# A two-layer cross-attention and FFN kernel: the first stage written out, its key projections four batches ahead of its query projections

## The reference

```python
x = x + _L0_xattn_ref(_layernorm(x), ctx_1024, ctx_1024, ...)   # q@Wq.T+bq, k@Wk.T+bk, v@Wv.T+bv, softmax over keys, @Wo.T+bo
x = x + _L0_ffn_ref(_layernorm(x), ...)                         # router over 32+8 experts, top 6, SiLU-gated experts
x = x + _L1_xattn_ref(_layernorm(x), ctx_1024, ctx_1024, ...)   # the same with -scale
x = x + _L1_ffn_ref(_layernorm(x), ...)                         # 256 -> 704 -> 256, activations and weights rounded to FP4 blocks
```

## Time and profile before

| | us |
|---|---|
| median of 3 runs | 1002.08 (996.93 to 1007.60) |
| the profiled execution, its own time | 1005.61 |
| its span, first to last instruction | 1003.8 |
| PE busy | 898.1 (89%) |
| DVE busy | 626.4 (62%) |
| ACT busy | 437.4 (44%) |
| POOL busy | 304.1 (30%) |

### The profile page before, as it was taken

One profiled execution on the slowest core, in us unless ns is written; L12 is line 12 of the kernel. 1 busy time (PEld: TensorE's weight loads), 2 busy tenths in 40 slices (PEclk: granted clock), 3 DMA queues, 4 the chain that ended last, 5 costly groups with the idle time before them and its releaser, 6 DMA issues.

```text
span 1003.8 us, 19829 instructions
## 1 busy us (share of the span) xinstructions
PE 898.1 (89%) x7228; PEld 685.1 (68%) x7228; DVE 626.4 (62%) x1317; ACT 437.4 (44%) x946; POOL 304.1 (30%) x311
## 2 busy tenths in 40 slices
PE   2997799999997978999999967799999996699996
PEld 1764687878876747878888844587878874366664
DVE  3455577878854594545545465566777764678872
ACT  0442466666664561111111112466666675345442
POOL 8003466767782260000000004000000001476673
PEclk9998799999998798999999977999999999999998
DMA  9788644444333469121111204345565500000000
GB/s 258 219 238 203 113 93 92 93 93 93 62 106 98 138 214 250 46 67 32 32 32 48 65 3 82 74 85 112 107 117 109 106 27 21 0 11 16 16 10 22
DMA packets 98157, 90.45 MB, mean 90 GB/s; under 512 B 43554, under 2 KB 85410, under 8 KB 97954
## 3 DMA queue, kind: packets, MB, share of 16 engines
q1 hardware_dynamic: 98066, 89.25, 36.6%
HBM read 69.36 MB, written 19.63 MB: 89 GB/s over the span
## 4 chain that ended last, share of the span: by engine, by line
PE 72%; DVE 12%; DMA 5%; POOL 3%; ACT 3%; issue 2%; SPq 2%; DVEq 0%; POOLq 0%; ACTq 0%
PE ps L988 13%; PE ps L805 8%; PE ps L859 8%; PE ps L791 8%; PE ps L994 7%; PE ps L819 7%; PE ps L1062 3%; DMA Qz<-mT 3%; PE ps L709 3%; PE ps L1078 2%; PE ps L868 2%; POOL Pr L645 2%; PE ps L779 2%; PE ps L828 1%; DMA X<-x_in 1%
## 5 line engine op out<-in xcount | busy, mean ns | idle before, releaser
L1444 DVE TENSOR_REDUCE ext<-ps 112x2 f32<-112x750 f32 x256 | 232.6, 933 | 66.5 <-PE ps L791 63.4
L1175 ACT ACTIVATE Pr<-ps 125x448 f32<-125x448 f32 x384 | 199.2, 542 | 88.5 <-PE ps L805 75.0
L805 PE MATMUL ps<-Qz,Kp 98*125 98x224 f16 x768 | 130.7, 265 | 14.0 <-DMA Qz<-mT 11.7
L791 PE MATMUL ps<-Kp,Qz 96*112 96x375 f16 x512 | 122.6, 332 | 5.8 <-DMA Qz<-qscr 4.9
L805 PEld LDWEIGHTS ps<-Qz,Kp 98*125 98x125 f16 x768 | 94.8, 137 | 47.2 <-DMA Qz<-mT 15.9
L859 PE MATMUL ps<-wv,ctx 128*125 128x256 f32 x384 | 120.7, 400 | 1.9 <-DVE xT L1417 1.0
L599 POOL TENSOR_TENSOR X<-X,bo 112x256 f32 x32 | 22.5, 724 | 284.6 <-DVE Pr L1362 233.0
L1585 DVE TENSOR_TENSOR Pr<-Pr,ps 128x336 f32<-128x336 f32 (+2 forms) x86 | 32.7, 381 | 88.9 <-ACT Pr L1257 73.8
L819 PE MATMUL ps<-Pr,Vx 125*32 125x112 f32 x3072 | 86.9, 261 | 0.0
L819 PEld LDWEIGHTS ps<-Pr,Vx 125*32 125x32 f32 x3072 | 71.4, 110 | 14.9 <-ACT Pr L1175 10.3
L1589 DVE SCALAR_TENSOR_TENSOR X<-ps,W,X 112x256 f32<-112x256 f32 x167 | 70.7, 477 | 17.3 <-PE ps L994 17.3
(11 more groups left out here) (176 smaller groups left out, 1417.1 us busy)
## 6 DMA issues: line engine op xcount, KB each, us to landing
ctx<-ctxT SPq DMA_DIRECT2D x56, 375.0 KB, 3.7
Kp<-kscr SPq DMA_DIRECT2D x96, 187.5 KB, 4.8
kscr<-ksp SPq DMA_DIRECT2D x24, 375.0 KB, 4.2
Pr<-wexp SPq DMA_DIRECT2D x20, 384.0 KB, 4.2
Qz<-qscr SPq DMA_DIRECT2D x174, 28.0 KB, 4.1
expert<-wexp SPq DMA_DIRECT2D x12, 384.0 KB, 3.9
Pr<-ctxT SPq DMA_DIRECT2D x8, 375.0 KB, 4.5
kscr<-Pr SPq DMA_DIRECT2D x8, 375.0 KB, 3.9
```

The lines of the kernel that those rows point to most:

```text
L791: last = mm(ps[0:S, 2 * (p % 2) + u, 0:M], Qz[0:96, q0 + u * S:q0 + (u + 1) * S], Kp[0:96, k0:k0 + M], start=True, stop=True)
L805: last = mm(ps[0:KC, 4 + k % 2, u * 2 * S:(u + 1) * 2 * S], Kp[0:98, k0:k0 + KC], Qz[0:98, q0:q0 + 2 * S], start=True, stop=True)
L1175: A(Pr[g % 2][0:KC, j, GI * t:GI * t + GI, :].rearrange("r h q -> r (h q)"), ps[0:KC, 4 + k % 2, 0:GI * S], ACT.Exp, scale=scale).then_inc ...
L1444: V.tensor_reduce(ext[0:S, 2 * p:2 * p + 2], ps[0:S, 2 * (p % 2):2 * (p % 2) + 2, 0:M], AX_X, red).then_inc(row_maximum_taken, 1)
```

## The change

It does the following.

1. SP's opening order becomes `wk`, `bqk`, contexts 0 and 1, x, `wq`. PE and ACT wait only for `wk` and `bqk` before the first keys; the query weights have their own semaphore.
2. The loop is written out. PE does K(0) to K(3), T(0), T(1), and then for each g Q(g), K(g+4), T(g+2). ACT and DVE follow the same order; DVE does KL(0) and KL(1) ahead of the statistics of x.
3. SP's order for each b becomes: store keys of b+3, load the context of b+5, store queries of b. Stores of keys and of queries have semaphores of their own. `wv`, `wo`, `bv`, `bo` of layer 0 come in b = 0, 1, 2. `load_kq(0)` stands after the store of queries 8, `load_kq(1)` after that of queries 11.
4. After Q(12) to Q(15), PE does two `score_rows` of batch 0 each, DVE two `row_maximum` each. PE_FIRST holds no R any more.
5. The later weights (3,324 KB, without layer 0's) are issued one batch at a time after `load_kq(b+3)` in the first attention. `scale_weights` and with it the rounding run one batch later; the last batch's turn takes pieces 14 and 15.

Its core (semaphores, the unchanged parts of helpers, and the same edit repeated are left out):

```diff
-PE_FIRST = "R R V V R V V R W R W R R R M"
+PE_FIRST = "V V V V M W W"
+LEAD = 4
...
-        NW0, NW = 16 * 3, 16 * (4 + 7 + 3)
+        NWK, NW, NL = 16 * 2, 16 * 4, 16 * (7 + 3)
...
             weight(wk[0], attn[0]["wk"], first_weights_loaded)
-            load_ctx(0, 0)
+            sp.dma_start(bqk[0][:, :], attn[0]["bqk"]).then_inc(first_weights_loaded, 16)
+            load_ctx(0)
+            load_ctx(1)
             sp.dma_start(X[:, :], x).then_inc(x_loaded, 16)
-            weight(wq[0], attn[0]["wq"], first_weights_loaded)
-            sp.dma_start(bqk[0][:, :], attn[0]["bqk"]).then_inc(first_weights_loaded, 16)
-            load_ctx(1, 1)
+            weight(wq[0], attn[0]["wq"], query_weights_loaded)
...
+            def load_next_ctx(b):
+                if b < B:
+                    sp.wait_ge(keys_projected, b)
+                    load_ctx(b)
...
+            def load_late_weights(b):
+
+                if b == 0:
+                    load_gate_or_up(0, fg, gate_weights_loaded)
+                elif b == 2:
+                    load_gate_or_up(1, fu, up_weights_loaded)
...
+            def store_keys(b):
                 for ready in (keys_high_ready, keys_low_ready):
-                    sp.wait_ge(ready, n)
+                    sp.wait_ge(ready, b + 2)
...
-                    sp.wait_ge(keys_projected, 2)
-                    load_ctx(2, 0)
-                    with sp.Fori(0, B // 2 - 2) as i:
-                        for par in (0, 1):
-                            sp.wait_ge(keys_projected, i * 2 + (par + 3))
-                            load_ctx(i * 2 + (par + 3), 1 - par)
-                            store_keys(i * 2 + par, i * 2 + (par + 2), par)
-                            store_queries(i * 2 + par, i * 2 + (par + 2), par)
...
+                    load_next_ctx(2)
+                    load_next_ctx(3)
+                    store_keys(0)
+                    store_keys(1)
+                    load_next_ctx(4)
+                    store_keys(2)
+                    for b in range(B):
+                        if b + 3 < B:
+                            store_keys(b + 3)
+                        load_next_ctx(b + 5)
+                        store_queries(b)
+                        if b < 3:
+                            load_outer_weights(0, b, weights_loaded)
+                        if b == 8:
+                            sp.wait_ge(padding_set, 7)
+                            sp.wait_ge(split_keys_stored[0], 16)
+                            sp.wait_ge(split_queries_stored[0], 16)
+                            load_kq(0)
+                        elif b == 11:
...
+                            load_kq(1)
+                        elif b == 12:
+                            for p in (0, 1):
+                                sp.wait_ge(keys_projected, B + p)
+                                load_values_ctx(p, p)
                     for par in (0, 1):
-                        sp.wait_ge(split_stored[par], 32 * (B // 2) + 16)
+                        sp.wait_ge(split_keys_stored[par], 16 * (B // 2))
+                        sp.wait_ge(split_queries_stored[par], 16 * (B // 2))
                     load_kq(2)
...
-                    if l == 1:
+                    if l == 0:
+                        load_late_weights(b)
+                    else:
                         relay(b)
                     flatten(b + 1)
...
# tensor engine
+                    for g in range(LEAD):
+                        project_keys(g)
+                    turn_x(0, 0)
+                    turn_x(1, 1)
+                    pe.wait_ge(query_weights_loaded, 16)
+                    for g in range(B):
+                        project_queries(g, g % 2)
+                        project_keys(g + LEAD)
+                        turn_x(g + 2, g % 2)
+                        if g == B - LEAD:
...
+                            keys_here(0)
+                        if g >= B - LEAD:
+                            score_rows(0, 2 * (g - B + LEAD))
+                            score_rows(0, 2 * (g - B + LEAD) + 1)
...
# scalar engine
+                    if g >= 2:
+                        act.wait_ge(split_queries_stored[par], 16 * (g // 2))
...
# vector engine
+                if l == 0:
+                    dve.wait_ge(first_weights_loaded, NWK)
+                    keys_low(0)
+                    keys_low(1)
+                    dve.wait_ge(x_loaded, 16)
                 norms(False, 0, B if l == 0 else QG)
...
+                    for g in range(B):
+                        if g + 3 < B:
+                            dve.wait_ge(x_is_turned, g + 3)
+                            layer_norm(g + 3, xn[1 - g % 2]).then_inc(x_normalised, 1)
+                        queries_low(g, g % 2)
+                        keys_low(g + LEAD)
+                        if g >= B - LEAD:
+                            row_maximum(0, 2 * (g - B + LEAD))
+                            row_maximum(0, 2 * (g - B + LEAD) + 1)
...
-                        elif step == "q" and l == 0:
-                            scale_weights(b, next(steps))
+                        elif step == "q" and l == 0 and b > 0:
+                            k = next(steps)
...
+                            scale_weights(b - 1, k)
+                            if b == B - 1 and k == 2:
+                                for k in range(3):
+                                    scale_weights(B - 1, k)
```

More of the change, by code:

```diff
@@ L235, in build @@
         queries_low_ready = sem("queries_low_ready")
[L236 removed]
+        split_keys_stored = [sem(f"split_keys_stored{p}") for p in (0, 1)]
+        split_queries_stored = [sem(f"split_queries_stored{p}") for p in (0, 1)]
         kq_loaded = [sem(f"kq_loaded{r}") for r in range(NR)]
@@ L701, in _, with project_keys @@
             values_begun, outs_begun = 0, 0
-            def project_keys(l, g, par, nctx):
-                pe.wait_ge(ctx_loaded[par], nctx)
-                wait_from(pe, keys_low_ready, g)
-                for m in range(C2):
-                    for c in range(C2):
-                        last = mm(ps[:, 4 * l + 2 * par + m, 0:M], wk[l][:, c, 128 * m:128 * m + 128],
-                                  ctx_sb[par][:, c, :], start=(c == 0), stop=(c == C2 - 1))
-                last.then_inc(keys_projected, 1)
+            def project_keys(g):
+                if g < B:
+                    pe.wait_ge(ctx_loaded[g % 2], 16 * (g // 2 + 1))
+                    if g >= 2:
+                        pe.wait_ge(keys_low_ready, g)
+                    for m in range(C2):
+                        for c in range(C2):
+                            last = mm(ps[:, 2 * (g % 2) + m, 0:M], wk[0][:, c, 128 * m:128 * m + 128],
+                                      ctx_sb[g % 2][:, c, :], start=(c == 0), stop=(c == C2 - 1))
+                    last.then_inc(keys_projected, 1)
             for l in (0, 1):
@@ L729, in project_queries @@
                     pe.wait_ge(xT_copied, g + 1)
-                    if not (isinstance(g, int) and g == 0):
+                    if g >= 2:
                         pe.wait_ge(queries_low_ready, g)
@@ L1112, in _, with keys_high @@
             A = nc.scalar.activation
-            def keys_high(l, g, i, par):
-                act.wait_ge(keys_projected, g + 2)
-                act.wait_ge(split_stored[par], i * (32 - 16 * l) + (32 * (B // 2 * l) + 16))
-                for m in range(C2):
-                    last = A(ksp[par][:, m, 0, :], ps[:, 4 * l + 2 * par + m, 0:M], ACT.Identity,
-                             bias=bqk[l][:, 2 + m:3 + m])
-                last.then_inc(keys_high_ready, 1)
+            def keys_high(g):
+                if g < B:
+                    act.wait_ge(keys_projected, g + 2)
+                    if g >= 2:
+                        act.wait_ge(split_keys_stored[g % 2], 16 * (g // 2))
+                    for m in range(C2):
+                        last = A(ksp[g % 2][:, m, 0, :], ps[:, 2 * (g % 2) + m, 0:M], ACT.Identity,
+                                 bias=bqk[0][:, 2 + m:3 + m])
+                    last.then_inc(keys_high_ready, 1)
             for l in (0, 1):
@@ L1142, in _ @@
                 if l == 0:
[L1143 removed]
+                    for g in range(LEAD):
+                        keys_high(g)
                     x_turned(0, 0)
                     x_turned(1, 1)
[L1146 to L1154 removed]
+                    for g in range(B):
+                        queries_high(g, g % 2)
+                        keys_high(g + LEAD)
+                        x_turned(g + 2, g % 2)
                     act.wait_ge(weights_loaded, NW)
@@ L1483, in _ @@
                 if l == 0:
-                    dve.wait_ge(ffn_weights_loaded, 16 * 5)
-                    dve.wait_ge(padding_set, 7)
-                if l == 0:
-                    for p in range(PAIRS):
-                        row_maximum(g0, p)
+                    for b in (0, 1):
+                        layer_norm(b, xn[b]).then_inc(x_normalised, 1)
```

(8 more changed lines are left out.)

179 lines of the change are left out of this document (76 added, 103 removed).

## The result

The changed kernel takes 1008.89 us (median of 19 runs, 1004.66 to 1015.88), the kernel before 1002.26 (19 runs, 996.93 to 1007.6). The ratio is 1.0075, with a 95% interval of 1.0054 to 1.0096: slower by 0.5 to 1%. Forecast were 1007 us and a range of 994 to 1014.

A forecast was written before the change was run, and what follows sets the result against it. It took PE to bound the first stage at 3.63 us per batch, after the wait for x. Profiled 1005.6 plus 3.6 (first C) plus 1.5 (tail) gave 1010.7, on the median's scale 1007 us; range 994 to 1014.

The forecast's parts named there:

- three batches of keys won in the wait for x: First stage's opening: three key batches, 7.6 us of PE, done in idle time; the whole gain.
- the ring does not bind: Rival, chance 0.12: key loop does not wait on the store-and-load ring; first C about 99, median scale 997 us.
- The start: Opening through K(4): statistics of x at 16.0, LN(0) at 25.1, K(4) ends at 32.3, 1.0 us later.
- The ring: Key loop: context load behind key store makes two batches take 9.81 us against 7.26; takes back 12.8 us.
- `load_kq(0)`, which I gave nothing: SP in the key loop: its 4.8 us lie where SP waits for KL(12) anyway; cost nothing.
- The clock, given no part of the sum: Ring's idle times: a clock fall would double K; set aside because PE works 7.3 of every 9.8 us.
- The last queries: Last four query batches: stores behind load_kq(1), queries 12 landed 94.2, last store 102.0; first C 109.1, 3.6 us later.
- What moving the row scores saves is hidden: Before the first C: moving batch 0's row scores saves nothing; store, reload, flatten set the way to C.
- The cover that I named: Before the first C: values and the split lie beside the store and load_kq(2), hiding what moving row scores saves.
- PE starts C at half rate, as now: First C: PE idles over 9 us ahead of it and starts at half rate, as before.
- The later weights: First attention: issuing them after load_kq(b+3) costs nothing; up to 1 us each time if a flatten landed behind.
- The tail: Rounding's end before the router: one more DVE stall beside POOL and later copies, 1.5 us, bounds 0 and 4.2.

The follow-up runs named there:

- E1: Changed kernel with SP's load of context b+5 put ahead of the store of keys b+3: 1000.79 us, ratio 0.9988 to the kernel before.
- E0: The changed kernel again, no edit, for a second trace: 1010.54 us, ratio 1.0072 to the kernel before.
- E10: The changed kernel a third time, no edit, for a third trace: 1009.63 us.
- E6: Changed kernel with batch 0's row scores and maxima back after the last queries, first attention items ordered by hand: 1015.57 us, ratio 1.0123 to the kernel before.
- E5: Changed kernel with context load before key store, weight pieces back in place, SP's end re-ordered, load_kq(0) spread over four steps: 995.63 us, ratio 0.9933 to kernel before.
- E8: E5 with load_kq(1) also spread, over steps 10 to 13: 992.99 us, ratio 0.9892 to the kernel before.
- E2: Changed kernel with the last FFN's gate weights loaded in the first stage and piece b scaled in turn b again: 1006.69 us, ratio 1.004 to kernel before.

## Why the prediction was right, and where it was not

**The verdict came from the right place.** A ring of store and load on SP takes back more than the three batches of keys won in the wait for x. The rows show each link, and E1, which opens that link and nothing else, gives 9.75 us back. The rival "the ring does not bind" is excluded, and its price was too low by 2 to 4 us: it put the first C of such a kernel at 99 and the median at 997; E1 has 101.2 and 1000.8.

**The start.** Statistics at 15.57 (forecast 16.0), first normalised batch at 24.63 (25.1), K(4) done at 32.14 (32.3). The sum of its first part held, not its split: K(0) waited for its context until 5.99, and K(0) and K(1) together were done at 13.42 (forecast 13.7).

**The ring.** Between K(6) and K(12) two batches take 9.37, 9.46 and 9.25 us, forecast 9.81. The context landed in 3.9 us and not in 4.2. K(15) started at 82.49, forecast 82.5. That agreement is luck twice over. The other two traces have 88.07 and 87.78. And in this one two terms were off against each other: the quiet rings were some 0.4 us shorter each, and **`load_kq(0)`, which I gave nothing, cost the two rings in which it lies 1.6 and 2.5 us** (K(11) to K(13) 11.03, K(12) to K(14) 11.88). Nor did K(15) wait for its own context there: it started 3.72 us after K(14), at PE's pace, so the ring of the even batches set it, where the forecast had followed the odd ones. Timeline of SP:

```profile
67.45 0.46 SPq L371 DMA_DIRECT2D ctx<-ctxT  x1
...
68.58 2.47 SPq L446 DMA_DIRECT2D Kp<-kscr  x3
71.08 2.82 SPq L456 DMA_DIRECT2D Qz<-qscr  x6
74.41 0.38 SPq L427 DMA_DIRECT2D kscr<-ksp  x1
74.84 0.46 SPq L371 DMA_DIRECT2D ctx<-ctxT  x1
```

The prediction looked only at SP's time, 4.8 us, and said that SP waits for KL(12) anyway. Two things were left out. Context 13 was issued at 67.45, just ahead of the nine small-packet loads, and TensorE took it 5.5 us later, where the quiet ones were taken 3.7 to 4.0 us after their issue (context 7, beside the last weights of layer 0, 4.6). And Kp's three issues took 2.47 us, not 1.6, so that store and context 14 went out behind them.

**The clock, given no part of the sum.** The prediction named the danger and set it aside, because PE still works 7.3 of every 9.8 us. In E0 it is 5.8 us, all of the 5.6 by which K(15) is later than in the first trace; in E10 it is 1.7 of 5.3, and the rest stays open; in the first trace it is nothing. On the mean of the three it is 2.5 us, and the first C is at 110.1, where 109.1 was forecast. A share of busy time did not tell. Nor did the length of a wait by itself: of the ten waits of 1.7 us and more in the three traces four were followed by the lower clock (1.72, 2.27, 3.07 and 4.36 us), and six, of 1.83 to 2.20 us, were not. In E6's trace a wait of 2.59 us passed, and in E5's one of 2.13 did not. What decides it no run here shows.

**The last queries.** Queries 14 waited for the store of queries 12 until 94.00; the landing was forecast for 94.2. The last store then landed in some 2 us, where the sum had 4.0, and `load_kq(2)` went out at 99.67, not 102.0. That is the 2 us between the forecast 109.1 and the first trace's 107.10.

**"What moving the row scores saves is hidden": wrong.** The sum did not suffer, since it was made with the scores in their new place. But the part was put at nothing, and it is worth about 5 us: 15.7 less 10.0 to 10.5 from the last queries to the first C, and 0.005 of the ratio, 5 us, by E6, which ran in another set than the changed kernel. The cover that I named was `load_kq(2)`, out at 102.63 in the kernel before, behind whose issue the maxima, copied at 99.96, do hide. That was read from a kernel in which the last queries came 11 to 15 us sooner. In the changed one they come at 97 to 101, and had the scores stayed behind them, the maxima and not `load_kq(2)` would have set the flatten. Of three parts, then (the keys ahead, the row scores, the rounding one batch later), one loses by its order on SP, one wins 5 us that I did not see, and one costs 2.8.

**"PE starts C at half rate, as now": wrong in two traces of three.** The first four matmuls of C take 0.60 us in the first trace and in E0, 1.00 in E10 and 1.01 before. The granted clock then stays at 1.00 in the first trace and falls to 0.50 from 113 to 116 us in E0. The stretch to copy 1 is 8.6 us in the first trace and 10.3 and 11.4 in the others, against 11.3 and 11.0. Why the traces differ here was not tested.

**The later weights.** Nothing in the attention: 172.6 to 173.8 us from copy 1 to copy 15 in all traces but E8's, as forecast. The tail was forecast at 1.5 us with bounds of 0 and 4.2, by one more stall; it is 2.8, by three. E2 takes it away exactly. In the changed trace four operations of the chain are long: TENSOR_SCALAR on uint32 at 0.67 and 1.53 us, SCALAR_TENSOR_TENSOR at 1.44 and TENSOR_TENSOR at 1.61, where 0.17 or 0.18 is what they take undisturbed, and each ends within 0.1 us of one of POOL's. The Trainium skill, "SBUF — State Buffer", section "Who interferes with whom", says that a DVE operation with two inputs in SBUF contends with a GpSimd one that reads SBUF, and so does one in a two-port mode. The trace agrees for those with two inputs; no run shows in which mode the two TENSOR_SCALARs ran.

**Against the sum**: first C +4.7 (forecast +3.6), the first turn −1.1 (0), the tail +2.8 (+1.5), together +6.4 where +5.1 was forecast.

## What to carry to other kernels

A queue that issues in order makes a dependence of every neighbour: when a load that frees the next step is put behind a store that waits for this step's result, two short waits become one ring, and its length, not the busiest engine, is the pace. Write that ring down link by link; then ask of every burst of issues in it not only what it takes of the queue's time but what lands late beside it.

When an edit is put at nothing because something else covers it, check the cover in the changed schedule, not in the old one. And compare traces by the stretches that the edit touches: here the last stretch, which nobody changed, scattered by 5 us, nearly as much as the whole effect.

## What the runs showed that I had not expected

TensorE's lower clock in a loop that is 80% busy (47.47 of 59 us): groups of eight matmuls at 4.3 to 5.4 us instead of 2.7 to 2.8, in two of three traces of the changed kernel and in neither of the two before. They came also in loops with the ring open, where a single wait of 4.17 us was followed by 4.48 us (E1).

A single DVE chain of 16-element operations, 5.4 us with one stall beside POOL, became 8.2 us with three more, although POOL's work did not grow, it only came later.
